# The edge preparation of a graph network reordered: earlier loads, source one-hots first, ScalarE given packing and multiplies

## The reference, cut to what matters

```python
edge_index = jnp.stack([src, dst])
x = _layernorm(x + _L0_gnn_ref(x, edge_index, ...), axis=-1)
x = _layernorm(x + _L1_gnn_ref(x, edge_index, edge_attr_4, node_vec1, edge_weight1, ...), axis=-1)
x = _layernorm(x + _L2_gnn_ref(x, edge_attr_16, ..., src, dst, edge_type_90), axis=-1)
x = _layernorm(x + _L3_gnn_ref(x, edge_index, edge_type_8, ...), axis=-1)
...
# in L2, of the edge attributes he only this is used:
z_e = he @ Ws.T
e = jnp.concatenate([z_src, z_e, z_dst], axis=1) @ Wa.T
```

## Time and profile before

| | us |
|---|---|
| median of three runs | 8562.17 |
| lowest and highest of them | 8555.83, 8563.68 |
| the profiled execution, its own time | 8550.26 |
| its span in the profile | 8548.6 |
| first block, until DVE starts on the second | 18.86 |
| second block, until DVE starts on the third | 91.46 |
| first scatter of POOL | 184.26 |
| last scatter starts | 1222.0 |

### The profile page before, as it was taken

How to read it: one execution, slowest core, us unless ns; L and a number is a source line. 1 busy time by engine, 2 the same in 40 slices (tenths; PEclk the granted TensorE clock), 3 DMA queues, 4 the chain that set the end, 5 groups by cost and what they waited for, 6 DMA issues and landing times. The chain is left out here.

```text
span 8548.6 us, 233535 instructions
## 1 busy us (share of the span) xinstructions
PE 6428.4 (75%) x55142; PEld 5292.3 (62%) x55143; DVE 4918.4 (58%) x13561; ACT 2820.3 (33%) x8471; POOL 5192.9 (61%) x7408
## 2 busy tenths in 40 slices
PE   1222215767699998999899989997866666888998
PEld 1111113555477776888688868886455555887998
DVE  7333345867455655666466646664322223998999
ACT  1222212545333333333333333332133333222554
POOL 2777754756477766777577757774277775222554
PEclk8555556555599999999999999998555555999999
DMA  2000003434388886888688878885200001332232
GB/s 66 3 3 3 3 29 104 120 97 120 88 221 216 216 197 181 222 221 222 161 222 222 222 164 223 222 222 121 95 7 7 7 7 24 82 82 57 73 73 59
DMA packets 1319112, 1000.54 MB, mean 117 GB/s; under 512 B 479354, under 2 KB 1223183, under 8 KB 1318092
## 3 DMA queue, kind: packets, MB, share of 16 engines
q1 hardware_dynamic: 941322, 649.30, 27.7%
q0 software_dynamic: 134272, 178.98, 10.8%
q10 hardware_dynamic: 243392, 170.76, 6.9%
HBM read 951.88 MB, written 54.19 MB: 118 GB/s over the span
## 5 line engine op out<-in xcount | busy, mean ns | idle before, releaser
L1480 POOL DMA_INDIRECT qg<-q_tab,qidx x2520 | 2389.2, 948 | 940.1 <-issue 699.2
L1635 DVE COPY ps<-b 128x384 f32<-128x384 f32 x1120 | 628.0, 561 | 1381.2 <-ACT h L1600 1374.8
L1067 PE MATMUL ps<-rhs_i,ohi 128*128 128x128 f32 (+2 forms) x8640 | 1215.7, 266 | 210.1 <-issue 197.2
L1067 PEld LDWEIGHTS ps<-rhs_i,ohi 128*128 128x128 f32 (+1 forms) x8640 | 1000.4, 163 | 342.5 <-issue 282.0
L1033 POOL COPY near<-x 128x48 bf16 x2160 | 675.9, 351 | 789.4 <-PE ps L1056 434.0
L1195 POOL DMA_INDIRECT got_m<-y_tab,idx_m x832 | 815.8, 981 | 478.8 <-issue 251.4
L1549 PE MATMUL ps<-ohm,h 128*128 128x128 f32 x6720 | 1032.9, 290 | 65.3 <-DVE ps L1635 33.9
L1549 PEld LDWEIGHTS ps<-ohm,h 128*128 128x128 f32 x6720 | 838.8, 192 | 257.7 <-issue 242.8
L1593 ACT ACTIVATE h<-ps,b 128x384 f32<-128x384 f32 x1120 | 650.2, 581 | 1052.2 <-PE ps L1531 955.6
L375 POOL DMA_INDIRECT list_by_src<-ring,rpos x808 | 783.1, 969 | 349.0 <-issue 255.0
L1212 PE MATMUL ps<-rhs_m,ohi_m 128*128 x2880 | 668.1, 403 | 416.1 <-ACT rhs_m L1238 387.3
(11 more groups left out here) (442 smaller groups left out, 8623.6 us busy)
## 6 DMA issues: line engine op xcount, KB each, us to landing
pb<-p_tab ACTq DMA_DIRECT2D x1680, 96.0 KB
pb<-p_tab SPq DMA_DIRECT2D x1680, 96.0 KB
places<-place_by_turn SPq DMA_DIRECT2D x560, 192.0 KB
places_i<-place_by_meeting SPq DMA_DIRECT2D x360, 256.0 KB, 3.4
places_i<-place_by_meeting SPq DMA_DIRECT2D x720, 128.0 KB, 3.1
qb<-q_tab SPq DMA_DIRECT2D x840, 64.0 KB
qg<-q_tab,qidx POOLq DMA_INDIRECT x2520
nears<-near_by_turn SPq DMA_DIRECT2D x560, 64.0 KB
```

The source lines that it names most:

```text
L1067: m = pe.matmul(ps[:, bass.ds(to[j], width)], ohi[:, h, j, :], rhs[:, h, j, 0:width], start=False, stop=True, skip_group_check=True)
L1480: pool.indirect_dma_start(qg[:, h, j, :], None, q_tab, IndirectOffsetOnAxis(ap=qidx[:, h, j:j + 1], axis=0)).then_inc(m_got[h], 16)
```

## The change

- First block: the two small weight loads leave at once, back to back, and DVE waits for these two alone; the loads of `x` and `nodev` follow behind their own memsets and are waited for only when the first layer starts (`s_x`).
- Second block: SP's index and type loads wait for the four tails of their arrays, ACT's loads for two tails, and the fill of `list_s` for the pad. The large tail of `ea16` moves from DVE to POOL, and SP's loads of `ea16` wait for it.
- DVE waits for sources and targets alone, builds all of `ohs` here (four instructions over 202 columns in place of eight over 101 in the third block), and packs the rest afterwards.
- ACT packs `dstt`, `ew` and `ea4` into the record and multiplies every quarter of `ea16`, one instruction per attribute (16 to a quarter). POOL sums quarters 2 and 0, DVE quarters 3 and 1.
- The third block keeps `ohd` alone.

```diff
                 @block.sync
                 def _(sp):
-                    sp.wait_ge(s_init, 1)
                     with nc.allow_non_contiguous_dma(reason="small weights"):
-                        sp_dma(sp, sp.dma_start(ws[:, :], a["L2_gnn_Ws"]), 16)
...
+                        sp.dma_start(ws[:, :], a["L2_gnn_Ws"]).then_inc(s_wsa, 16)
+                        sp.dma_start(wa[:, :], ...).then_inc(s_wsa, 16)
+                        sp.wait_ge(s_init, 1)
+                        sp.dma_start(x[:, 0:N // P, :], ...).then_inc(s_x, 16)
...
-                    dve.wait_ge(sp_dma.sem, n_dma)
+                    dve.wait_ge(s_wsa, 32)
...
+            ohs = sb("ohs", [P, Q, J, KS], BF16, st)
...
+                        pool.memset(ea16[P - 32:P, TAIL:T, :], 0.0).then_inc(s_tails16, 1)
+                        pool.wait_ge(s_tails16, 1)
...
-                        for q in (2, 3):
+                        for k, q in ((0, 2), (1, 0)):
                             lo, hi = q * TQ, (q + 1) * TQ
-                            pool.wait_ge(s_ea[q], 16 * len(by_edge(ea16, a["edge_attr_16"], lo, hi)))
-                            p_chain(pool, pool.tensor_tensor(ea16[:, lo:hi, :], ea16[:, lo:hi, :],
-                                                             a_rows[:, 0:1, :].to_broadcast([P, TQ, FIN]), ALU.mult))
+                            pool.wait_ge(s_times, k + 1)
...
-                        sp.wait_ge(s_pad, 1)
+                        sp.wait_ge(s_tails, 4)
...
-                                    sp.dma_start(d, v_).then_inc(s_load, 16)
+                                    sp.dma_start(d, v_).then_inc(s_load if t in (srct, dstt) else s_type, 16)
+                            sp.wait_ge(s_tails16, 1)
...
-                        act.wait_ge(s_pad, 1)
+                        act.wait_ge(s_tails4, 2)
...
+                            act.wait_ge(s_pad, 1)
...
+                        act.wait_ge(s_load, 2 * 3 * 16)
+                        act.activation(rec[:, :, 1], dstt[:, :], ACT.Copy).then_inc(s_pack, 1)
+                        act.wait_ge(s_ew, 2 * 3 * 16)
+                        act.activation(rec[:, :, 2], ew[:, :], ACT.Copy).then_inc(s_pack, 1)
+                        act.activation(rec[:, :, 3:7], ea4[:, :, :], ACT.Copy).then_inc(s_pack, 1)
+                        for q in (2, 0, 3, 1):
+                            lo, hi = q * TQ, (q + 1) * TQ
+                            act.wait_ge(s_ea[q], 16 * len(by_edge(ea16, a["edge_attr_16"], lo, hi)))
+                            for f in range(FIN):
+                                m = act.activation(ea16[:, lo:hi, f], ea16[:, lo:hi, f], ACT.Copy, scale=a_rows[:, 0, f:f + 1])
+                            m.then_inc(s_times, 1)
...
-                        v_chain(dve, dve.memset(srct[lastp, TAIL:T], 1 << 20))
...
-                        v_chain(dve, dve.memset(ea16[lastp, TAIL:T, :], 0.0))
+                        for t, none in ((srct, 1 << 20), (dstt, 1 << 20), (t8, 0), (t90, 0)):
+                            dve.memset(t[lastp, TAIL:T], none).then_inc(s_tails, 1)
...
-                        dve.wait_ge(s_load, 4 * 3 * 16)
+                        dve.wait_ge(s_load, 2 * 3 * 16)
...
+                        for j in range(J):
+                            dve.tensor_tensor(ohs[:, :, j, :], iota_b[:, None, :].to_broadcast([P, Q, KS]),
+                                              sbf[:, j * Q:(j + 1) * Q][:, :, None].to_broadcast([P, Q, KS]), ALU.is_equal)
...
-                        for q in (0, 1):
+                        for k, q in ((2, 3), (3, 1)):
                             lo, hi = q * TQ, (q + 1) * TQ
-                            dve.wait_ge(s_ea[q], 16 * len(by_edge(ea16, a["edge_attr_16"], lo, hi)))
-                            v_chain(dve, dve.tensor_tensor(ea16[:, lo:hi, :], ea16[:, lo:hi, :],
-                                                           a_rows[:, 0:1, :].to_broadcast([P, TQ, FIN]), ALU.mult))
+                            dve.wait_ge(s_times, k + 1)
                             v_chain(dve, dve.tensor_reduce(rec[:, lo:hi, 7], ea16[:, lo:hi, :], AX.X, ALU.add))
+                        dve.wait_ge(s_pack, 3)
...
-                            dve.tensor_tensor(ohs[:, lo:lo + HQ, j, :], iota_b[:, None, :].to_broadcast([P, HQ, KS]),
-                                              sbf[:, j * Q + lo:j * Q + lo + HQ][:, :, None].to_broadcast([P, HQ, KS]),
-                                              ALU.is_equal).then_inc(s_ohs, 1)
```

More of the change, by code:

```diff
@@ L146, in by_edge @@
             return pairs
+        s_x = sem("s_x")
         with ExitStack() as st:
@@ L154, in gnn_kernel @@
             b_pe, b_fpe = to_pe.base(1), from_pe.base(1)
-            s_init = sem("s_init")
+            s_init, s_wsa = sem("s_init"), sem("s_wsa")
             with nc.Block() as block:
@@ L183, in _ @@
                     v_chain(dve, dve.memset(x[:, :, :], 0.0))
+                    dve.memset(nodev[:, :], 0.0).then_inc(s_init, 1)
                     v_chain(dve, dve.memset(nothing[:, :], 0.0))
@@ L186, in _ @@
                     v_chain(dve, dve.memset(ones16[:, :], 1.0))
-                    dve.memset(nodev[:, :], 0.0).then_inc(s_init, 1)
-                    dve.wait_ge(sp_dma.sem, n_dma)
+                    dve.wait_ge(s_wsa, 32)
                     v_chain(dve, dve.tensor_scalar(wab[:, 0, :], ones16[:, :], wa[:, 1:2], None, ALU.mult))
@@ L224, in gnn_kernel @@
                 ti = sb("ti", [P, T], I32, sa)
-                tk = sb("tk", [P, T], I32, sa)
                 ew = sb("ew", [P, T], F32, sa)
@@ L234, in gnn_kernel @@
                 s_col = sb("s_col", [P, 3], F32, sa)
-                s_pad, s_load, s_ew, s_fill, s_rows = sem("s_pad"), sem("s_load"), sem("s_ew"), sem("s_fill"), sem("s_rows")
+                s_pad, s_load, s_type, s_ew, s_fill, s_rows = (sem("s_" + n) for n in ("pad", "load", "type", "ew", "fill", "rows"))
+                s_tails, s_tails4, s_tails16 = (sem("s_" + n) for n in ("tails", "tails4", "tails16"))
+                s_pack, s_times = sem("s_pack"), sem("s_times")
                 s_ea = [sem(f"s_ea{q}") for q in range(4)]
@@ L284, in _ @@
                         lastp = slice(P - 32, P)
-                        v_chain(dve, dve.memset(srct[lastp, TAIL:T], 1 << 20))
[L286 to L290, removed]
-                        v_chain(dve, dve.memset(ea16[lastp, TAIL:T, :], 0.0))
+                        for t, none in ((srct, 1 << 20), (dstt, 1 << 20), (t8, 0), (t90, 0)):
+                            dve.memset(t[lastp, TAIL:T], none).then_inc(s_tails, 1)
+                        dve.memset(ew[lastp, TAIL:T], 0.0).then_inc(s_tails4, 1)
+                        dve.memset(ea4[lastp, TAIL:T, :], 0.0).then_inc(s_tails4, 1)
                         v_chain(dve, dve.memset(padt[:, :, :], 0.0))
@@ L345, in gnn_kernel @@
             rpos = sb("rpos", [P, 2, 2 * J], I32, st)
-            s_ohs, s_ohd, s_cnt, s_evd, s_eva = (sem("s_" + n) for n in ("ohs", "ohd", "cnt", "evd", "eva"))
+            s_ohd, s_cnt, s_evd, s_eva = (sem("s_" + n) for n in ("ohd", "cnt", "evd", "eva"))
             s_sum, s_two = sem("s_sum"), sem("s_two")
@@ L389, in _ @@
                             if q % HQ == 0:
-                                pe.wait_ge(s_ohs, J * (q // HQ + 1))
                                 pe.wait_ge(s_ohd, J * (q // HQ + 1))
@@ L1378, in _ @@
                         if layer == 0:
+                            dve.wait_ge(s_x, 64)
                             v_chain(dve, dve.tensor_scalar(eps[:, :], eps[:, :], 1.0, None, ALU.add))
```

22 lines of the change are left out of this document (9 added, 13 removed).

## The result

The changed kernel took 8511.7 us, the median of four executions (8510.3 to 8517.71), against 8562.92 for the kernel before in the same session (8555.83 to 8571.49): the ratio is 0.9941, with an interval of 0.9924 to 0.9958, so 36 to 65 us less. A second session with twelve executions of the kernel before gave 0.9937 (0.9925 to 0.9950). The forecast was 8512, 50 us less.

The account below looks back on a forecast made before the run. The three preparation blocks run in series, so their time is paid in full; DVE bounds the third. Gains of 22.4 (first two blocks) and 27.5 us (third), about 50, taken off the 8562.17 median, gave 8512, range 8499 to 8530.

Parts of the forecast that it names:

- multiplies over 0.47 us: Second block, ACT: sign that would show the forecast wrong; multiplies were expected near 0.4 us.
- a load of attributes that leaves after 13: Second block, SP's queue: sign that would show the forecast wrong; the attribute loads were expected to leave at 11.9.
- First block: First block: DVE's product moves from 16.02 to 3.0, 13.0 us earlier; the second block's first memset to 5.9.
- Loads: Second block: first load leaves at 7.1, 21.6 us earlier; attributes at 11.9, first quarter lands at 32.7, last at 55.4.
- rival E: Second block: SP stays behind POOL's tail memset of 10.4 us, attributes leave 4.4 us late; gain 48, time 8514; chance 5%.
- rival B: Second block: sources and targets need the full 18.1 us, DVE ends 8.1 later; gain 42, time 8520; chance 15%.
- the ACT term: Second block: 0.40 us a multiply, 6.4 us a quarter, under the 7.5 between arrivals; ACT's path with DVE's sum ends at 65.3.
- rival A: Second block: ACT is the bound if a multiply costs 0.58 us or more; end 73.9, gain 45, time 8517; chance 12%.
- DVE: Second block: DVE, with POOL's additions costing 10.1 us among its instructions, finishes its work at 61.5 and sets the end.
- Third block: Third block: eight comparisons of 3.44 us leave DVE, the bound there; 27.5 us gained.
- my sum: Preparation: DVE sets the second block's end, 69.1; gains 22.4 + 27.5 = 49.9 us, time 8512; chance 50%.
- rival D: Later stages: 134 us more at TensorE's lower clock would turn the gain into a loss, time 8579; chance 2%.

Follow-up runs that it names:

- e6: Changed kernel with ACT multiplying 8 of 16 attributes in quarters 3 and 1, DVE the rest, x and nodev loads behind edge loads: 8507.4 us, 0.9943.
- e7: As e6, but DVE takes 8 attributes in quarter 3 alone, ACT all of quarter 1: 10454.13 us (0.9967), repeated 10603.22 us (0.9959).
- e1: Changed kernel with the source one-hots moved back to the third block: 8534.64 us, 0.9968.
- the probe: 66 extra ACT operations of 202 numbers on scratch tiles in the first block, to price each form; no kernel time given, 0.275 us both packed.
- e2: Changed kernel with the attribute multiplies back on POOL and DVE, ACT only packing: 8520.06 us, 0.9954.
- before_again: The kernel before the change, unaltered, profiled a second time: 8555.0 us, one execution.
- e4: Changed kernel with the loads back in their old order and waits, and the attributes' tail memset back on DVE: 8517.28 us, one execution.
- again: The changed kernel repeated without alteration: 8509.56 us, 0.9937 of the kernel before.
- third: The changed kernel repeated without alteration a third time, in a session where every kernel took over 10.4 ms: 10447.47 us, 0.9963.

## Why the prediction was right, and where its sum was not

The time, 8511.7, is the forecast's 8512, and the direction and range hold. The way there was partly another one, and two of the signs that the forecast itself named as wrong came true: multiplies over 0.47 us, and a load of attributes that leaves after 13.

**First block: right.** The product came 12.8 us earlier (13.0 forecast). The second block began at 6.79, not 5.9. SP was issuing `nodev` until 6.18, and the blocks meet for all engines; with those loads moved away (e6, e7) the first index load leaves at 7.36 instead of 8.07.

**Loads: right in kind, 1 to 3 us short.** The first index load left 20.6 us earlier, not 21.6, and the attributes at 13.59, not 11.9: the issue of the types took 3.22 us instead of 2.45. POOL's tail took 4.08 us, the lower of my two ends, and SP never waited for it, so rival E falls. The indices were there at 16.46 (17.1 forecast), which rules out rival B. The first quarter came at 35.65, not 32.7: 1.7 us of that is the later issue, and from issue to first use it took 22.06 us where it had taken 20.81 (33.49 to 54.30, rows 3 and 4), which nothing here explains; in e1, with the same loads, it came at 33.83.

**The failed step is the ACT term**: 0.40 us a multiply, "near the interpolation". It is 0.53. The interpolation gave the packed form exactly (357 ns against 356), but it was a duration, not the spacing in a row (0.275), which made it 0.08 too high; the read 64 bytes apart adds 0.17 and the scale from a tile 0.09, which makes 0.53. The bounds I gave, 0.36 and 0.60, held it; my choice of the one lay on the wrong side of the point that decides.

At 0.53 sixteen take 8.5 us, more than the 7.5 between arrivals, so all 64 run in a row, and the case is **rival A**, to which I gave 12%: its end was forecast at 73.9 and measured at 73.78, its gain at 45 us, and the preparation gained 45.5. The threshold written there, 0.58 us, was too high by the rival's own mechanism: ACT falls behind the arrivals from 7.5 / 16 = 0.47, and its end passes the sum's 69.1 from (69.1 - 0.5 - 3.5 - 32.7) / 64 = 0.51. The arrivals were near the 7.5: in e6, where ACT waits again, the last quarter was there at 55.54, 22 us behind the first, 7.3 each. Of the two arguments against A, "the two forms fit a straight line" says nothing, since any two do; and the other is an estimate that the probe bears out for packed operands, which these are not. The rival's match in the end is partly luck: it had a first quarter 3 us earlier and multiplies 0.05 us dearer.

**DVE: right in its rows, wrong in its role.** The four comparisons took 27.30 us (27.5 forecast) and DVE was through at 56.07, not 61.5, because POOL's additions, waiting for ACT, came at 44.17 and 55.33 instead of 39.1 and 46.6, the second round behind DVE's work. So none of the comparisons was lengthened, where the forecast had at least one. The exclusion was there (3.98 us for a shift of 0.58), but e1 shows that it wasn't in the way. The copy of 7.58 us, with which the forecast bore out the lock for two inputs, has one input only; the rows for two are the multiplies, 5.06 and 7.08 before, and e2's comparisons.

**Third block: right.** 27.8 us less, 27.5 forecast.

**The total.** The preparation gained 45.5 us (47.3 against before_again) where my sum had 49.9; the medians say 51, with intervals of 36 to 65 and 43 to 64, which hold both. That the total agrees with my sum to 1 us is chance. Single executions differ more than these terms: from the first scatter to the last layer norm, the same code throughout, the profiles took 8348.6 (e4) to 8371.1 us (again), 22 us apart. One such place can be seen in windows of 10 us between the third and the fourth layer norm (us; busy PE, PEld, DVE, ACT, POOL; granted clock; DMA share; GB/s), first after, then before:

```profile
7780.00:7790.00 10.00, 10.00 (x12) 0.96 (x12) 0.00 (x0) 1.36 (x2) 0.00 (x0) 0.50 0.00 0
```

```profile
7820.00:7830.00 10.00, 10.00 (x22) 1.35 (x20) 0.00 (x0) 3.38 (x5) 0.00 (x0) 1.00 0.00 0
```

Twelve matmuls in 10 us at the granted clock 0.50 (1.2 GHz) against 22 at 1.00 (2.4 GHz). The profiled execution of after lost 9 us of its lead between these two norms (41.6 us at the third, 32.6 at the fourth). That is the mechanism of rival D at a small size, but *again* kept its lead there (30.3 and 29.8) and had lost 9 us between the first norm and the second (43.0 and 34.1), so this place is not an effect of the change; what decides between executions stays open.

## What to carry to other kernels

Price an instruction that is new on an engine by its own form: whether it reads packed or apart, where its scale comes from, and how closely it follows the one before. When a sum turns on a threshold (here 7.5 us between arrivals over 16 instructions), work the threshold out and ask on which side each end of the price lies; that was worth more than the price's middle. Two parts of a change can be worth little apart and much together: free one engine only where another part fills it.

## What the runs showed of the hardware

ACT spaces 202-number operations at 0.275 us packed, 0.44 when the read is 64 bytes apart, and 0.53 (kernel) to 0.57 (probe) with both sides apart and a scale from a tile. DVE's sum of 16 numbers over 202 places takes 3.52 us when the 16 lie together and 5.8 to 5.9 when they are 808 bytes apart.

SP can be held while it issues a load behind others that have not landed. The second load of `x` (3.3 KB) shows it, first in the kernel before, then in the changed kernel; its row in e6_shared stands above:

```profile
8.95 0.28 SPq L175 DMA_DIRECT2D x<-in_x_dram  x1
```

```profile
2.25 1.54 SPq L176 DMA_DIRECT2D x<-in_x_dram  x1
```

It takes 0.28 us where the load ahead of it has landed, 1.54 right behind the first load of `x`, and 40.29 where the edge loads are under way too (39.15 and 40.38 in e7's two profiles). In e6 and e7 it did no harm, since nothing waits on SP's queue there. Ahead of the edge loads it does a little: SP is busy with `x` and `nodev` until 6.18, and the second block starts at 6.79, against 6.07 in e6.

In the two 10-ms sessions every kernel was slower, the one before too (10485.98 and 10650.22 us). The preparation kept its times (first scatter 139.6 in third); the edge stage did not. One window in it, in third and then in the changed kernel's first profile, with the columns as above:

```profile
3000.00:3100.00 100.00, 77.64 (x594) 65.78 (x595) 42.35 (x160) 25.11 (x47) 48.15 (x51) 0.85 0.54 148
```

```profile
3000.00:3100.00 100.00, 95.92 (x856) 79.49 (x856) 59.52 (x222) 35.71 (x67) 71.36 (x76) 1.00 0.81 216
```

In the same stretch of time 51 gathers instead of 76, and 148 GB/s instead of 216; the DMA engines are busy for a smaller share, 0.54 instead of 0.81, and the granted clock has a mean of 0.85 instead of 1.00. The gathers themselves are no dearer for POOL (944 ns each in third, 948 in the first profile), but POOL waits for its indices 1624.6 us in all instead of 230.7. Which resource is slower there, and whether it is the chip, wasn't tried, and stays open.
